# A mixture-of-experts and attention kernel: one copy placed ahead of an exponential, rows added a step sooner, and four transfers moved to another queue

## The chip, the cores and the metric

The kernel runs on one core of a Trainium2 chip. The metric is device time in microseconds (us) from the start to the end of one execution; lower is better. The page and the rows below come from one execution taken by the hardware profiler. PE is TensorE (matrix products), DVE is VectorE, ACT is ScalarE, POOL is GpSimd, and SP is SyncE, which here only issues DMA transfers.

## The reference

The input `x` has 8 sequences of 1024 tokens with 256 numbers each. It is normalised, and two branches work on the result:

```
xn = layernorm(x)
q, k, v = split(xn @ w_qkv)                    # 16 heads of 64
attn = softmax(causal(q @ k.T / sqrt(64))) @ v @ w_out
ffn  = sum over the two best experts of gate * (relu(xn @ w1[e] + b1[e]) @ w2[e] + b2[e])
out  = x + attn + ffn
```

An expert takes at most 2048 of the 8192 tokens. All is float32. Most products are made of three, of a rounded high part and the rest (`h` and `l` at the end of a tile's name).

## The kernel before

The program has stages one after the other: normalising and routing, the experts (up to about 900 us), and then attention, which adds all parts and is where the whole change lies. Attention runs over 64 **units** (`UNITS`): a unit is one pair of heads of one sequence, so 8 units make a sequence. A unit has 20 **steps**, and every engine goes through (unit, step) in the same order, with semaphores between the engines.

- A unit's 8 rows of 128 queries are done in 5 **rounds** of 4 steps (`ROUNDS`): rows (3,2), (4,1), (5,0), (6), (7). For a row, PE makes the scores S (L1231), DVE masks them, writes them to `pr` and finds the extreme `negm` (L1356), ACT takes the exponential in place (L1294), and a round later DVE makes reciprocals (L1362) and POOL scales the rows (L1438).
- The scaled rows have to be turned before they multiply the values. Rows 0 to 3 are turned by PE in 128x128 blocks into a PSUM bank (L1187), and ACT copies them out to `pT` (L1284). These pieces are called **turns**: `t30`, `t31`, `t20`, `t21` (row, head) and `t1`, `t0`. Rows 4 to 7 are turned by DVE in small squares (L1400, tile `squares`), and then DMA transfers, 16 for each group of two rows, place them in `pT`: `place` on SP's queue (L1085), `place_rest` on POOL's (L1467). Group 2 is rows 4 and 5, group 3 rows 6 and 7. In one unit SP issues 16 transfers of group 2 and 12 of group 3, and POOL 4 of group 3.
- PE multiplies by the values in three runs (L1264): groups 0 and 1, group 2, and group 3, at steps 3, 7 and 15 of the next unit.
- Beside this PE makes other **pieces**, each into one of three shared PSUM banks `W0`, `W1`, `W2`: `p0` to `p3` (queries and keys of the next unit, L1142), `v0`, `v1` (values, L1157), `xn` (L1165), and `o0` to `o3` (output products, L1176). The step of each piece on PE, ACT and DVE, and its bank, are written out by hand in the tables `STEP_OF`, `ACT_STEP`, `DVE_STEP`, `BANK_OF`. A piece waits until the piece before it in the same bank has been read. At steps 8 to 10 the order on PE is `t30` (W1), `t31` (W2), `t20` (W0), `t21` (W1), `o1` (W2), `p1` (W0), `o2` (W1).
- POOL's own work has a table too, `POOL_AT`. `split_w` and `split_wv` divide the next weights in high and low parts; `wvl` of `split_wv`, in every second unit, is what `v0` of the next unit needs, and `wl` lets SP load the next weights. `fetch`, `weigh`, `add` and `total` fetch a token's two expert rows, weigh and add them, and add the sum to `res` (L1502). DVE adds the output products to the same `res` (L1382), so the DVE addition for the same query group waits for `total`.

Of the kernel before, what the change touches and what calls it, by code (L numbers as in the profile page):

```python
# [845 lines left out]
def attention_and_sum(nc, k, x, xn_dram, w_qkv, w_out, pick, y_dram, out, start):  # L846
# [3 lines left out]
    UNITS = BATCH * PAIRS  # L850
# [7 lines left out]
    QUARTERS = P // BL  # L858
# [28 lines left out]
               "t30": 8, "t31": 8, "t20": 8, "t21": 8, "o1": 9, "p1": 10, "o2": 11,  # L887
               "p0": 12, "t1": 13,
               "t0": 16, "p2": 16, "p3": 17, "o3": 18}
    ACT_STEP = {"v0": 2, "xn": 2, "v1": 6, "t30": 8, "t31": 8, "t20": 9, "t21": 9, "p1": 12,  # L890
                "p0": 12, "t1": 13, "t0": 16, "p2": 17, "p3": 18}
    DVE_STEP = {"xn": 3, "o0": 6, "o1": 10, "p1": 12, "o2": 12, "p0": 15, "p2": 19, "p3": 19, "o3": STEPS + 2}
    BANK_OF = {"v0": 0, "xn": 1,
# [15 lines left out]
    RUN_OF = {g: j for j, groups in enumerate(RUN_GROUPS) for g in groups}  # L909
# [6 lines left out]
                return n - later, j  # L916
        return None

    POOL_AT = {"split_w": 1, "place3": 4, "total": 5, "choose": 6, "fetch0": 8, "fetch1": 9, "weigh": 13, "add": 14, "split_wv": 17}

    turns_of = lambda i: [t for t in TURNS if i in [at[0] for at in TURNS[t]]]
    turn_unit = lambda n, t: n if t in STEP_OF else END_STEP[TURNS[t][0][0]][0]
# [21 lines left out]
    with ExitStack() as c:  # L944
# [86 lines left out]
        score, negmax, expd, scaled = (Count(sem(f"s_{n}"), len(ORDER)) for n in ("score", "negmax", "expd", "scaled"))  # L1031
        recip = Count(sem("s_recip"), len(ROUNDS))
        squared = Count(sem("s_squared"), 2 * len(SQUARED))
        placed = {2: Count(sem("s_placed2"), 16 * QUARTERS * QUARTERS), 3: Count(sem("s_placed3"), 16 * QUARTERS * (QUARTERS - 1))}
        pool_placed = Count(sem("s_pool_placed"), 16 * QUARTERS)
        pv = Count(sem("s_pv"), RUNS)
        ohi, olo = Count(sem("s_ohi"), RUNS), Count(sem("s_olo"), RUNS)
        filled = Pieces(sem("s_filled"), lambda name: True)
# [30 lines left out]
        @block.sync  # L1069
        def _(e):  # L1070
            def load_w(m):
                for c_ in range(MC):
                    e.dma_start(wr[:, 2 * c_:2 * c_ + 2], wv[m % PAIRS][:, c_, :, 0:2 * HDIM]).then_inc(wload.sem, 16)

            def load_wv(m):
                for c_ in range(MC):
                    e.dma_start(wvr[:, c_], wvv[m % (PAIRS // 2)][:, c_, :, 2 * HDIM:]).then_inc(wvload.sem, 16)

            def place(n, g):
                e.wait_ge(squared.sem, squared.at(n, 4 * g - 4))  # L1080
                if n > 0:
                    e.wait_ge(pv.sem, pv.at(n - 1, RUN_OF[g] + 1))
                for a in range(QUARTERS - (g == 3)):
                    for b in range(QUARTERS):
                        e.dma_start(*strip(g, a, b)).then_inc(placed[g].sem, 16)  # L1085

            def store(b, g):
                e.wait_ge(dve.sem, dve.at((b + 1) * PAIRS, f"o{g}"))
                e.dma_start(outv[:, b, 2 * g:2 * g + 2], res[:, 2 * g:2 * g + 2]).then_inc(stored[g].sem, 16)

            def refill(b, g):
                if b > 0:
                    e.wait_ge(stored[g].sem, stored[g].at(b - 1, 16))
                e.dma_start(res[:, 2 * g:2 * g + 2], xv[:, b, 2 * g:2 * g + 2]).then_inc(rload[g].sem, 16)

            e.dma_start(xnt[:], xnv[AHEAD]).then_inc(xload.sem, 16)
            load_w(1)
            load_wv(1)
            for n in range(UNITS):
                b, u = n // PAIRS, n % PAIRS  # L1100
                if n == 0:
                    e.wait_ge(s_wolo, 1)
                    for g in range(GROUPS):
                        refill(0, g)
                if n + 2 < UNITS:
                    e.wait_ge(wlo.sem, wlo.at(n, MC))
                    load_w(n + 2)
                if n + 1 + AHEAD < TILES:
                    e.wait_ge(filled.sem, filled.at(n, "xn"))
                    e.dma_start(xnt[:], xnv[n + 1 + AHEAD]).then_inc(xload.sem, 16)  # L1110
                if n > 0:
                    place(n - 1, 3)
                if b > 0 and u == 0:
                    for g in range(3):
                        store(b - 1, g)
                    for g in range(3):
                        refill(b, g)
                if n < UNITS - 1:
                    place(n, 2)
                if n % 2 == 0 and n // 2 + 2 < UNITS // 2:  # L1120
                    e.wait_ge(wvlo.sem, wvlo.at(n // 2, MC))
                    load_wv(n // 2 + 2)
                if b > 0 and u == 0:
                    store(b - 1, 3)
                    refill(b, 3)
            for g in range(GROUPS):
                store(BATCH - 1, g)
            for g in range(GROUPS):
                e.wait_ge(stored[g].sem, stored[g].at(BATCH - 1, 16))

        @block.tensor
        def _(e):
# [103 lines left out]
            def values(n, j):  # L1236
                groups = RUN_GROUPS[j]
                if in_squares(n, 2 * groups[0]):
                    g = groups[0]
                    e.wait_ge(placed[g].sem, placed[g].at(n + 1, 0))  # L1240
                    if g == 3:
                        e.wait_ge(pool_placed.sem, pool_placed.at(n + 1, 0))
                else:
                    for m, name in [(turn_unit(n, t), t) for g in groups for i in (2 * g, 2 * g + 1) for t in turns_of(i)]:
                        if by_act(name):
                            e.wait_ge(act.sem, act.at(m, name))
                        else:
                            e.wait_ge(dve.sem, dve.at(m, name))
                if j == 0:
                    e.wait_ge(act.sem, act.at(n // 2 * 2 - 1, "v1"))  # L1250
                    if n > 0:
                        e.wait_ge(olo.sem, olo.at(n - 1, RUNS))
                else:
                    e.wait_ge(act.sem, act.at(n // 2 * 2, "v1"))
                    e.wait_ge(olo.sem, olo.at(n, j))
                for g in groups:
                    KT, o0 = 2 * g + 2, g % 2 * GQ
                    for kt in range(KT):
                        a = P if kt == KT - 1 else 0
                        for h in range(2):  # L1260
                            hs = slice(h * HDIM, (h + 1) * HDIM)
                            vs = slice(n % 2 * P + h * HDIM, n % 2 * P + (h + 1) * HDIM)
                            turned_p = wide_of(g, h, kt, a // P) if in_squares(n, 2 * g) else pT[g][:, h, kt, a:GQ]
                            ins = e.matmul(O[hs, o0 + a:o0 + GQ], vv[n // 2 % 2][:, kt, vs], turned_p,  # L1264
                                           start=(kt == 0), stop=(kt == KT - 1))
                ins.then_inc(pv.sem, 1)
# [73 lines left out]
        def _(e):  # L1340
# [52 lines left out]
            def square(n, i, h):  # L1393
                g, KT = i // 2, i + 1
                if n > 0 and i % 2 == 0 and h == 0:
                    e.wait_ge(placed[g].sem, placed[g].at(n, 0))
                    if g == 3:
                        e.wait_ge(pool_placed.sem, pool_placed.at(n, 0))
                e.wait_ge(scaled.sem, scaled.at(n, SCALE_ORDER.index((i, h)) + 1))
                e.transpose(sq[g][:, :, 2 * h + i % 2, 0:KT, :],  # L1400
                            room_of(n, i, h)[:, OFFSET[i]:OFFSET[i] + KT * P].rearrange("p (k b i) -> p b k i", b=QUARTERS, i=BL)
                            ).then_inc(squared.sem, 1)
# [30 lines left out]
        def _(e):  # L1433
# [25 lines left out]
                for c_ in range(MC):  # L1459
                    e.tensor_tensor(wvl[:, c_], flat(wvr[:, c_]), wvh[:, c_].bitcast(F32), ALU.subtract).then_inc(wvlo.sem, 1)  # L1460

            def place_rest(n):
                e.wait_ge(squared.sem, squared.at(n + 1, 0))
                if n > 0:
                    e.wait_ge(pv.sem, pv.at(n - 1, RUN_OF[3] + 1))
                for b in range(QUARTERS):
                    e.dma_start(*strip(3, QUARTERS - 1, b)).then_inc(pool_placed.sem, 16)  # L1467

            def choose(m):
                if m > 0:  # L1470
# [35 lines left out]
            for n, s in ALL + END:  # L1506
                r, x = s // SUB, s % SUB
                m, q = back(n, s, SUB)[0], (r - 1) % len(ROUNDS)
                if x == 0 and 0 <= m < UNITS:
                    for j in range(FIRST[q], FIRST[q + 1]):  # L1510
                        scale(m, j)
                for name, at in POOL_AT.items():
                    if s != at:
                        continue
                    if name == "total" and n > 0:
                        total(n - 1)
                    if n == UNITS:
                        continue
                    if name == "place3" and n > 0:
                        place_rest(n - 1)  # L1520
                    elif name == "choose":
                        choose(n)
                    elif name == "split_w" and n + 1 < UNITS:
                        split_w(n)
                    elif name == "split_wv" and n % 2 == 0 and n // 2 + 1 < UNITS // 2:
                        split_wv(n // 2)
                    elif name[:5] == "fetch":
                        fetch(n, int(name[5]))
                    elif name == "weigh":
                        weigh(n)  # L1530
                    elif name == "add":
                        add(n)
# [38 lines left out]
```

## Time and profile before

| | |
|---|---|
| median of 3 runs | 2953.59 us (2950.54 to 2953.61) |
| profiled execution | 2948.78 us, its span 2947.0 us |
| mean granted PE clock | 0.989 of full speed |
| busy share PE / DVE / ACT / POOL | 96% / 71% / 58% / 55% |
| DMA | 371.58 MB, mean 126 GB/s |

The span runs from the first to the last instruction; the profiled execution's own time has 1.8 us more around it. A busy share is a mean over all stages. A timeline row gives the start, the length, and in square brackets the idle time of the engine just before it and what ended it. PE's products overlap, so the distance of two starts tells more of them than their length.

### The profile page before, as it was taken

The numbers are of one execution on the slowest core, as the hardware profiler recorded it, in microseconds if no ns is written. First come the engines' busy times: TensorE is split into PE (matmuls) and PEld (weight loads), VectorE is DVE, ScalarE is ACT, GpSimd is POOL, SyncE is SP. The second block draws the span as 40 slices with busy tenths as digits, with TensorE's granted clock in tenths as the row PEclk, the third lists the DMA queues.
The fourth block names the chain that finished last, engine by engine and source line by source line (L and its number), as shares of the span: only waits on it lengthen the run. The fifth ranks groups of instructions, "written<-read, shape, count | busy, mean of one in ns | idle before, by whom it ended". The sixth has DMA issues, their size and how long they took to land.

```text
span 2947.0 us, 61139 instructions
## 1 busy us (share of the span) xinstructions
PE 2825.5 (96%) x21321; PEld 2283.0 (77%) x21321; DVE 2091.7 (71%) x4448; ACT 1699.5 (58%) x3934; POOL 1606.8 (55%) x2379
## 2 busy tenths in 40 slices
PE   4599999999998999999999999999999999999998
PEld 3489999899997777777777777777777777777776
DVE  7843444434435888888888888888888888888886
ACT  3455444444444666666666666666666666666664
POOL 3122122221214767667667767667667767767674
PEclk8799999999999999999999999999999999999999
DMA  7022212222113555655655655565566557556553
GB/s 252 19 78 76 74 49 80 74 76 66 55 53 102 141 144 146 167 145 153 163 140 150 158 150 153 134 167 152 134 167 156 137 139 184 134 139 179 135 133 93
DMA packets 252806, 371.58 MB, mean 126 GB/s; under 512 B 77392, under 2 KB 177744, under 8 KB 252512
## 3 DMA queue, kind: packets, MB, share of 16 engines
q1 hardware_dynamic: 228096, 301.09, 38.5%
q0 software_dynamic: 24416, 66.65, 8.4%
q8 instruction: 174, 2.85, 0.4%
q14 instruction: 120, 0.98, 0.1%
HBM read 102.80 MB, written 33.55 MB: 46 GB/s over the span
## 4 chain that ended last, share of the span: by engine, by line
PE 62%; SPq 2%; DMA 2%; issue 1%; DVE 1%; ACT 1%; DVEq 0%; ACTq 0%
PE O L1264 17%; PE S L1231 15%; PE W L1142 12%; PE W L1157 7%; PE W L1176 6%; PE W L1187 5%; SPq L1085 2%; DMA pT<-squares 1%; DVE pr L1356 1%; DMA out<-res 0%; ACT pr L1294 0%; PE W L1165 0%; DVE squares L1400 0%; ACT pT L1284 0%; DVE res L1382 0%
## 5 line engine op out<-in xcount | busy, mean ns | idle before, releaser
L1438 POOL TENSOR_SCALAR pr<-pr,rinv 128x512 f32<-128x512 f32 (+7 forms) x1024 | 752.0, 750 | 535.1 <-DVE rinv L1362 528.9
L1294 ACT ACTIVATE pr<-pr,negm 128x512 f32<-128x512 f32 (+7 forms) x1024 | 786.7, 773 | 285.2 <-DVE negm L1356 285.2
L1356 DVE CUSTOM_DVE_ANT_0 pr<-S,late 128x512 f32<-128x512 f32 (+7 forms) x1024 | 717.5, 752 | 109.1 <-PE S L1231 107.6
L1264 PE MATMUL O<-pT,vv 128*64 128x256 f32 (+1 forms) x5120 | 540.3, 362 | 4.6 <-DMA pT<-squares 4.6
L1400 DVE STREAM_TRANSPOSE squares<-pr 128x640 f32<-128x640 f32 x504 | 495.0, 1020 | 0.0
L1264 PEld LDWEIGHTS O<-pT,vv 128*64 128x64 f32 x5120 | 345.8, 137 | 183.1 <-issue 18.9
L832 DVE TENSOR_TENSOR hl<-h,hh 128x512 fp32r<-128x512 f32 x256 | 192.7, 753 | 320.3 <-ACT hh L793 308.1
L789 ACT ACTIVATE h<-pH,b1c 128x512 f32<-128x512 f32 x256 | 176.0, 688 | 367.3 <-PE pH L719 336.9
L1284 ACT ACTIVATE pT<-W 128x512 f32<-128x512 f32 (+3 forms) x520 | 199.2, 437 | 214.8 <-PE W L1187 214.8
L731 PE MATMUL pY<-w2h,hh 128*128 128x256 f32 x1024 | 287.7, 281 | 2.5 <-DVE hl L832 2.5
L731 PE MATMUL pY<-w2l,hh 128*128 128x256 f32 x1024 | 288.9, 282 | 0.0
L731 PE MATMUL pY<-w2h,hl 128*128 128x256 f32 x1024 | 287.9, 281 | 0.0
L1142 PE MATMUL W<-xnh,wh 128*128 128x512 f32 x512 | 221.2, 432 | 23.5 <-issue 18.3
L1382 DVE TENSOR_TENSOR res<-W,res 128x512 f32<-128x512 f32 x256 | 175.7, 686 | 69.0 <-POOL res L1502 44.9
L1231 PE MATMUL S<-khf,qh 64*128 64x512 f32 (+2 forms) x1024 | 218.8, 422 | 2.8 <-DVE negm L1356 2.8
L719 PE MATMUL pH<-xh,w1h 128*128 128x512 f32 x512 | 205.5, 401 | 4.8 <-DVE xl L804 2.6
L1142 PE MATMUL W<-xnh,wl 128*128 128x512 f32 x512 | 202.5, 395 | 0.0
L1142 PE MATMUL W<-xnl,wh 128*128 128x512 f32 x512 | 202.3, 395 | 0.0
L719 PE MATMUL pH<-xl,w1h 128*128 128x512 f32 x512 | 201.7, 394 | 0.0
L719 PE MATMUL pH<-xh,w1l 128*128 128x512 f32 x512 | 201.5, 393 | 0.0
L1294 ACT ACTIVATION_READ_ACCUMULATOR pr<-pr,negm 128x1 f32 x1024 | 199.2, 195 | 0.0
L731 PEld LDWEIGHTS pY<-w2h,hh 128*128 128x128 f32 x1024 | 192.9, 188 | 7.9 <-issue 2.9
(176 smaller groups left out, 6221.7 us busy)
## 6 DMA issues: line engine op xcount, KB each, us to landing
pT<-squares SPq DMA_DIRECT2D x1008, 96.0 KB, 2.1
pT<-squares SPq DMA_DIRECT2D x756, 128.0 KB
pT<-squares POOLq DMA_DIRECT2D x252, 128.0 KB
y<-yb SPq DMA_DIRECT2D x128, 128.0 KB, 1.7
wr<-in_L_attn_w_qkv SPq DMA_DIRECT2D x128, 128.0 KB, 2.3
x<-in_L_attn_x SPq DMA_DIRECT2D x16, 512.0 KB, 9.1
xn<-xn SPq DMA_DIRECT2D x16, 512.0 KB, 4.4
w1r<-in_L_ffn_w SPq DMA_DIRECT2D x8, 1024.0 KB
```

Source lines behind the costliest of these rows:

```text
L719: ins = e.matmul(pH[hc % 4][:], w[par][:, m, ws], xx[q][:, m, :], start=(n == 0), stop=(n == 3 * MC - 1))
L731: ins = e.matmul(pY[t % 2][:], hs[q][:, hc, ts_], ws[par][:, hc, :], start=(hc == 0 and n == 0), stop=(hc == HC - 1 and n == 2))
L832: e.tensor_tensor(hl[q][:, hc, :], h32[hc % 2][:], hh[q][:, hc, :].bitcast(F32), ALU.subtract).then_inc(hlo.sem, 1)
L1142: ins = e.matmul(W, ws[:, 2 * m + of_k], xs[:, t0:t0 + HT, m, :], start=(i == 0), stop=(i == 3 * MC - 1))
L1157: ins = e.matmul(W[:, t * VW:(t + 1) * VW], xs[:, t0 + t, m, :], ws[:, m, :], start=(j == 0), stop=(j == len(terms) - 1))
L1231: ins = e.matmul(S[h][:, off + f * HALF:off + f * HALF + cols], t[hs, i * P:(i + 1) * P], u[f][n % 2][hs, 0:cols], start=(j == 0), stop=(j ...
L1264: ins = e.matmul(O[hs, o0 + a:o0 + GQ], vv[n // 2 % 2][:, kt, vs], turned_p, start=(kt == 0), stop=(kt == KT - 1))
L1284: ins = e.activation(dst, src, ACT.Copy) if by_act(name) else e.tensor_copy(dst, src)
L1294: e.activation(p, p, ACT.Exp, bias=negm[:, c0:c0 + 1], scale=-1.0, accum_out=rsum[:, c0:c0 + 1]).then_inc(expd.sem, 1)
L1356: e.tensor_tensor_reduce(room_of(n, i, h)[:, off:off + w], S[h][:, off:off + w], late[:, SEQ - w:], 1.0, -MASKED, ALU.add, ALU.min, negm[: ...
L1400: e.transpose(sq[g][:, :, 2 * h + i % 2, 0:KT, :], room_of(n, i, h)[:, OFFSET[i]:OFFSET[i] + KT * P].rearrange("p (k b i) -> p b k i", b=Q ...
L1438: e.tensor_scalar(p, p, rinv[:, c0:c0 + 1], 1.0, ALU.mult, ALU.mult).then_inc(scaled.sem, 1)
```

## The change

Three numbers of hand-written tables change, and one function takes over four transfers.

- ACT's step for `t20` goes from 9 to 8, which puts that copy ahead of the first exponential of round (5,0).
- POOL does `total` at step 4 and `place3` at step 5 (before, the other way round).
- A new entry `place2` at step 16 lets POOL issue the last four of group 2's transfers; SP's `place` then issues 12 of both groups. The two places that waited for POOL's transfers of group 3 wait for those of group 2 likewise.

```diff
-    ACT_STEP = {"v0": 2, "xn": 2, "v1": 6, "t30": 8, "t31": 8, "t20": 9, "t21": 9, "p1": 12,
+    ACT_STEP = {"v0": 2, "xn": 2, "v1": 6, "t30": 8, "t31": 8, "t20": 8, "t21": 9, "p1": 12,
...
-    POOL_AT = {"split_w": 1, "place3": 4, "total": 5, "choose": 6, "fetch0": 8, "fetch1": 9, "weigh": 13, "add": 14, "split_wv": 17}
+    POOL_AT = {"split_w": 1, "total": 4, "place3": 5, "choose": 6, "fetch0": 8, "fetch1": 9, "weigh": 13, "add": 14, "place2": 16, "split_wv": 17}
...
-                for a in range(QUARTERS - (g == 3)):
+                for a in range(QUARTERS - 1):
                     for b in range(QUARTERS):
                         e.dma_start(*strip(g, a, b)).then_inc(placed[g].sem, 16)
...
                     e.wait_ge(placed[g].sem, placed[g].at(n + 1, 0))
-                    if g == 3:
-                        e.wait_ge(pool_placed.sem, pool_placed.at(n + 1, 0))
+                    e.wait_ge(pool_placed[g].sem, pool_placed[g].at(n + 1, 0))
...
-            def place_rest(n):
-                e.wait_ge(squared.sem, squared.at(n + 1, 0))
+            def place_rest(n, g):
+                e.wait_ge(squared.sem, squared.at(n, 4 * g - 4))
                 if n > 0:
-                    e.wait_ge(pv.sem, pv.at(n - 1, RUN_OF[3] + 1))
+                    e.wait_ge(pv.sem, pv.at(n - 1, RUN_OF[g] + 1))
                 for b in range(QUARTERS):
-                    e.dma_start(*strip(3, QUARTERS - 1, b)).then_inc(pool_placed.sem, 16)
+                    e.dma_start(*strip(g, QUARTERS - 1, b)).then_inc(pool_placed[g].sem, 16)
```

On ACT, at steps 7 to 9 of the third unit, a row reads: line, operation, what it writes and reads (W0 to W2 are the shared banks, `pr` the rows), and the size. Before:

```order
L1325 ACTIVATE oh<-O 128x256
L1284 ACTIVATE pT1<-W1 128x4x128
L1284 ACTIVATE pT1<-W2 128x4x128
L1294 ACTIVATE pr0,rsum<-pr0,negm 128x768
L1284 ACTIVATE pT1<-W0 128x3x128
L1284 ACTIVATE pT1<-W1 128x3x128
L1294 ACTIVATE pr1,rsum<-pr1,negm 128x768
```

And after the change:

```order
L1324 ACTIVATE oh<-O 128x256
L1283 ACTIVATE pT1<-W1 128x4x128
L1283 ACTIVATE pT1<-W2 128x4x128
L1283 ACTIVATE pT1<-W0 128x3x128
L1293 ACTIVATE pr0,rsum<-pr0,negm 128x768
L1283 ACTIVATE pT1<-W1 128x3x128
L1293 ACTIVATE pr1,rsum<-pr1,negm 128x768
```

The copy out of W0 (`t20`) has passed one exponential of 768 columns; the copy out of W1 (`t21`) has stayed behind it.

On POOL, from the scaling of row 6 (896 columns) in a unit with `split_wv` to the next unit's step 6, before:

```order
L1438 TENSOR_SCALAR pr3<-pr3,rinv 128x896
L1457 TENSOR_SCALAR wvh<-wvr 128x256 x2
L1460 TENSOR_TENSOR wvl<-wvr,wvh 128x256 x2
L1438 TENSOR_SCALAR pr4<-pr4,rinv 128x1024
...
L1438 TENSOR_SCALAR pr1<-pr1,rinv 128x384
L1467 DMA pT3<-squares3 32x1024 x4
L1502 TENSOR_TENSOR res<-res,yg0 128x256
L1472 COPY sel<-pick 128x4
```

After the change, the same places in the program (the second part one unit earlier, where it reads the same):

```order
L1436 TENSOR_SCALAR pr3<-pr3,rinv 128x384
L1500 TENSOR_TENSOR res<-res,yg0 128x256
L1465 DMA pT3<-squares3 32x1024 x4
L1470 COPY sel<-pick 128x4
...
L1436 TENSOR_SCALAR pr3<-pr3,rinv 128x896
L1465 DMA pT2<-squares2 32x768 x4
L1455 TENSOR_SCALAR wvh<-wvr 128x256 x2
L1458 TENSOR_TENSOR wvl<-wvr,wvh 128x256 x2
L1436 TENSOR_SCALAR pr4<-pr4,rinv 128x1024
```

Four transfers of group 2 now stand between the scaling of row 6 and `split_wv`, and the addition to `res` has passed the four transfers of group 3.

## Rows read from the trace of the kernel before

**Rows 1.** The page, part 1: busy us (share of the span) and instructions
```profile
PE 2825.5 (96%) x21321; PEld 2283.0 (77%) x21321; DVE 2091.7 (71%) x4448; ACT 1699.5 (58%) x3934; POOL 1606.8 (55%) x2379
```

**Rows 2.** Waits from 928 to 2885 us: us in total, times, longest
```profile
DVE res L1382 <- POOL res L1502: 44.9, 16, 3.1
...
PE W L1142 <- issue: 18.3, 58, 0.3
...
PEld W L1176 <- ACT pT L1284: 11.1, 62, 0.2
...
PE O L1264 <- DMA pT<-squares: 4.6, 6, 1.8
```

**Rows 3.** Timeline of PE, the end of o1 and the start of p1
```profile
2031.16 0.28 PE L1176 MATMUL W<-woh,ol 128*128 128x256 f32 x1
2031.76 0.51 PE L1142 MATMUL W<-xnh,wh 128*128 128x512 f32 x1 [0.32 <-issue]
2032.11 0.39 PE L1142 MATMUL W<-xnl,wh 128*128 128x512 f32 x1
2032.34 0.40 PE L1142 MATMUL W<-xnh,wl 128*128 128x512 f32 x1
```

**Rows 4.** Timeline of ACT at the same steps
```profile
2029.33 1.09 ACT L1284 ACTIVATE pT<-W 128x512 f32<-128x512 f32 x2 [1.80 <-PE W L1187]
2030.30 0.94 ACT L1294 ACTIVATE pr<-pr,negm 128x768 f32<-128x768 f32 x1
...
2031.22 0.87 ACT L1284 ACTIVATE pT<-W 128x384 f32<-128x384 f32 x2
```

**Rows 5.** Timeline of PE, where v1 ends and o0 begins
```profile
2023.59 0.28 PE L1157 MATMUL W<-wvh,xnl 128*128 128x256 f32 x1
2023.70 0.28 PE L1176 MATMUL W<-woh,oh 128*128 128x256 f32 x1
```

**Rows 6.** Timeline of PE, first product of p1 in three units
```profile
2000.38 0.50 PE L1142 MATMUL W<-xnh,wh 128*128 128x512 f32 x1 [0.32 <-issue]
...
2660.52 0.50 PE L1142 MATMUL W<-xnh,wh 128*128 128x512 f32 x1 [0.32 <-issue]
...
2691.68 0.50 PE L1142 MATMUL W<-xnh,wh 128*128 128x512 f32 x1 [0.32 <-issue]
```

**Rows 7.** Line L1165 (xn): durations ns, first and last start
```profile
L1165 PE MATMUL W<-ident,xnt x110: 270/271/273, 921.2 to 2615.6; 128*128 128x128 f32 x110
```

**Rows 8.** Timeline of POOL around the places of the change
```profile
2011.28 0.78 POOL L1457 TENSOR_SCALAR wvh<-wvr 128x256 fp32r<-128x256 f32 x2
2012.14 1.45 POOL L1460 TENSOR_TENSOR wvl<-wvr,wvh 128x256 fp32r<-128x256 f32 x2
2017.10 2.23 POOL L1438 TENSOR_SCALAR pr<-pr,rinv 128x1024 f32<-128x1024 f32 x2 [3.51 <-DVE rinv L1362]
...
2019.79 0.78 POOL L1447 TENSOR_SCALAR wh<-wr 128x256 fp32r<-128x256 f32 x2
...
2024.98 2.09 POOL L1467 DMA_DIRECT2D pT<-squares  x4
2027.09 0.75 POOL L1502 TENSOR_TENSOR res<-res,yg 128x256 f32<-128x256 f32 x1
```

**Rows 9.** Timeline of DVE beside them
```profile
2011.36 1.23 DVE L1356 CUSTOM_DVE_ANT_0 pr<-S,late 128x1024 f32<-128x1024 f32 x1 [0.86 <-PE S L1231]
...
2013.65 2.10 DVE L1400 STREAM_TRANSPOSE squares<-pr 128x896 f32<-128x896 f32 x2
2015.68 0.65 DVE L1390 TENSOR_TENSOR ql<-W,qh 128x512 fp32r<-128x512 f32 x1
```

**Rows 10.** Timeline of PE, first product of v0
```profile
2016.43 0.39 PE L1157 MATMUL W<-wvh,xnh 128*128 128x256 f32 x1
```

**Rows 11.** Timeline of SP's queue: issues of groups 2 and 3
```profile
2008.25 10.23 SPq L1085 DMA_DIRECT2D pT<-squares  x16
...
2023.61 8.33 SPq L1085 DMA_DIRECT2D pT<-squares  x12
```

**Rows 12.** Issues from 928 us on, line L1085: us from issue to landing
```profile
DMA to landing us min/median/max: 2.0/2.1/3.9
```

**Rows 13.** Timeline of PE, first products with group 3's rows
```profile
2037.55 0.65 PE L1264 MATMUL O<-pT,vv 128*64 128x256 f32 x4
```

More of the change, by code:

```diff
@@ L1033, in attention_and_sum @@
         squared = Count(sem("s_squared"), 2 * len(SQUARED))
-        placed = {2: Count(sem("s_placed2"), 16 * QUARTERS * QUARTERS), 3: Count(sem("s_placed3"), 16 * QUARTERS * (QUARTERS - 1))}
-        pool_placed = Count(sem("s_pool_placed"), 16 * QUARTERS)
+        placed = {2: Count(sem("s_placed2"), 16 * QUARTERS * (QUARTERS - 1)), 3: Count(sem("s_placed3"), 16 * QUARTERS * (QUARTERS - 1))}
+        pool_placed = {g: Count(sem(f"s_pool_placed{g}"), 16 * QUARTERS) for g in (2, 3)}
         pv = Count(sem("s_pv"), RUNS)
@@ L1396, in square @@
                     e.wait_ge(placed[g].sem, placed[g].at(n, 0))
-                    if g == 3:
-                        e.wait_ge(pool_placed.sem, pool_placed.at(n, 0))
+                    e.wait_ge(pool_placed[g].sem, pool_placed[g].at(n, 0))
                 e.wait_ge(scaled.sem, scaled.at(n, SCALE_ORDER.index((i, h)) + 1))
@@ L1519, in _ @@
                     if name == "place3" and n > 0:
-                        place_rest(n - 1)
+                        place_rest(n - 1, 3)
+                    elif name == "place2" and n < UNITS - 1:
+                        place_rest(n, 2)
                     elif name == "choose":
```

## The prediction

> **What bounds the kernel now.** I read the page's busy shares first. PE is busy 96% of the span, the next engine, DVE, 71% [rows 1]. So time can only come from what PE still waits for, or from PE having less to do. The list of waits over the units of attention (928 to 2885 us) says how little that is [rows 2]: 18.3 us before L1142 in 58 places, put down to "issue"; 11.1 us of PE's weight loads before L1176, ended by a copy of ACT; 4.6 us before L1264 for the placing transfers. The longest wait of the four is DVE's: 44.9 us in 16 places for POOL's addition to `res`.
>
> Is PE the chain from unit to unit, so that a wait removed there shortens every unit? The trace has an experiment of its own. The piece `xn`, two small PE products, is there in 55 units and then no more: its last start is 2615.6 [rows 7]. The first product of `p1` stands 31.38 us apart in two units with it (2000.38 and 2031.76) and 31.16 apart in two without it (2660.52 and 2691.68) [rows 3, 6]. Two products less shorten the unit by 0.22 us, about two distances of 0.11 between such starts. PE's own time passes into the period one to one; nothing else holds a unit at 31.4.
>
> Then I looked at the 18.3 us in the timeline. The last product of `o1` starts at 2031.16, the first of `p1` at 2031.76 [rows 3]. `p1` writes bank W0, and the last user of W0 was `t20`, which ACT has to copy out. ACT copies `t30` and `t31` from 2029.33 on, does an exponential of 768 columns at 2030.30, and only at 2031.22 begins on `t20` and `t21`, two copies in 0.87 us [rows 4]. Half of that puts the end of `t20`'s copy near 2031.66, and PE starts 0.10 us later. The "issue" is this wait: each of the gaps of 0.32 stands at this place.
>
> **ScalarE's copy.** Moved ahead of the exponential, `t20`'s copy starts where the exponential did, at 2030.30, and ends near 2030.8. PE needs it at about 2031.3, so the wait is gone with 0.5 us to spare. What comes back: where a piece follows another with its waits fulfilled, the starts are 0.11 apart (2023.59 to 2023.70, the last of `v1` to the first of `o0`) [rows 5]. Here they are 0.60 apart, so 0.48 to 0.49 comes back. The first product after the gap costs more as well: 0.35 to the second, 0.23 from there to the third [rows 3], so another 0.11 to 0.12 if the stream isn't broken. Together 0.59 us in each unit with a `p1`, 63 units. The lower bound for this term is what the list counts as idle, 18.3 us in all [rows 2]; I take the distances of starts, since PE's ends are modelled and its starts are not.
>
> What is late instead? The first exponential ends some 0.45 us later. Behind it stands `t21`'s copy, which now alone follows it and so ends where it did, near 2032.1; the second exponential starts as before. `o2`, which needs W1 from `t21`, comes six products of 0.23 after `p1`, so from about 2032.7 on: 0.6 us of cover. The round's reciprocals wait for all its exponentials, and the last has not moved.
>
> **Does the gain stay?** PE comes 0.59 us earlier to everything behind `p1`. The next wait that could catch it is group 3's run at 2037.55 [rows 13]. SP issues these transfers until 2031.94 (2023.61 + 8.33) [rows 11], and they land 2.1 us later [rows 12], at about 2034.0. That leaves 3.5 us, of which the change takes 0.59. At the borders between sequences, where SP stores and reloads `res` too, there is no room: the 4.6 us in 6 places are just these [rows 2]. There are 7 borders. At each the 0.59 us is given back as a longer wait for group 3, whose issues begin with the squares of row 7, which nothing moves. So 63 - 7 = 56 units count: 56 x 0.59 = 33.0 us. DVE's part of the loop, from the scores of row 7 to `v0`, is tight (`ql` runs until 2016.33, `v0` starts at 2016.43 [rows 9, 10]), but it begins after an idle 0.86 us that PE's scores end, so it moves with PE.
>
> **The sum of expert rows.** `total` now runs 2.09 us sooner, the length of the four issues that it passes [rows 8]. DVE's 44.9 us in 16 places, 2.8 each, shrink to about 0.7 each, 34 us of DVE's time in all. PE gets nothing of it: the list shows no wait of PE for these additions, and the gap before `p1` is there all the same. Value 0, hidden under PE's products. Group 3's four transfers of POOL start 0.75 us later [rows 8], at 2025.7, and are issued by 2027.9, still 4 us ahead of SP's last. Cost 0.
>
> **Four transfers of group 2 to POOL.** SP's 16 issues of 10.23 us become 12, so it is done 2.5 us sooner; group 2's run had been waiting for nothing. Value 0 in most units. POOL pays four issues: beside other DVE work they took 2.09 us [rows 8]. They fall behind the scaling of row 6, from 2011.3 to 2013.4, and group 2's squares have long been there (SP began on them at 2008.25 [rows 11]). Behind them stand `split_wv` in 31 units and the scaling of row 7. `split_wv` takes 2.31 us and ended at 2013.59; now 2015.7, while `v0` needs it at 2016.43: 0.7 us of cover is left. Row 7's scaling waits for DVE until 2017.10 anyway, with 3.51 us idle before it. Cost 0, but the cover is thin.
>
> The profile has no plain issue of POOL beside DVE's squares of row 6. From below, 0 us on the path at 2.09 us for the four. From above, POOL may be held until DVE's unbroken run ends, 2013.65 + 2.10 = 2015.75 [rows 9]. What speaks against the upper end: two small POOL operations at 2011.28 beside DVE's minimum took 0.78 us, the same as two of their size at 2019.79 beside other DVE work [rows 8, 9]. I take 2.09. The Trainium skill has a rule that speaks against this edit: "SBUF — State Buffer", section "SBUF: two separate sides", says that a DMA issued from GpSimd has its descriptors written by that engine, which is locked out of the shared port while VectorE runs an operation in a two-port mode, so that the transfer seems blocked by it. By that rule the sum would be that of the last rival below, if DVE's operations here are of that kind; by the rows it is 33.0 us gained.
>
> **The sum.** 33.0 + 0 + 0. The profiled execution took 2948.8 us, so its like would be 2915.8. The median of the runs shown is 4.8 above it, so against that 2953.6 - 33.0 = 2920.6; I say 2920.
>
> **The rivals.**
> - Only the counted idle comes back, because `p1`'s first product stays slow: 18 us, 2935. For it: the first product of `p1` may need its pause for another reason. Against it: [rows 5]. Chance 0.13.
> - More comes back. SP's four issues fewer and the DMA queue emptied sooner also take away the waits at the borders: 63 x 0.59 + 4.6 = 42 us, 2912. Against it: at a border SP waits for stores of `res` in between, so it reaches group 3 no sooner. Chance 0.13.
> - The gap moves. PE comes sooner and stands before group 3's run in all units, or another chain holds the period. That needs transfers landing 3 us later than now, or a chain that the step of 0.22 with `xn` would have shown. Time within 3 us of 2952. Chance 0.08.
> - Slower: POOL's four issues are held by DVE. They end at 2015.75, `split_wv` at 2018.06, `v0` is 1.7 us late in 31 units: 53 us lost against 33 gained, 2974. It decides from a price of 3.9 us for the four issues on (2.84 us from the end of `wvl` to `v0`, and 33 / 31 = 1.06 more). Chance 0.07.
>
> My forecast has 0.55, between 2915 and 2926; 0.04 is left to mixtures, mostly on the fast side.
>
> **How the numbers follow.** A measurement of this kernel tells about 0.2%, 6 us, from no change. Faster: 0.55 + 0.13 + 0.13 and 0.03 of the mixtures, 0.84. Same 0.09, slower 0.07. The range takes in the first three cases, from 2910 to 2937, and leaves out some 0.2.
>
> **What would show it.** Right: in the profile after, `p1` starts 0.11 to 0.12 after the last product of `o1`, its second product 0.23 later, the "issue" row before L1142 has shrunk from 18.3 us to nearly nothing, and units are 30.8 us apart. PE's wait for group 3 at the borders is longer, 4.6 + 7 x 0.59, about 9 us. DVE's wait for `total` is near 11 us. POOL's eight plain issues in a unit take about 0.52 us each, and SP issues 12 and 12. Wrong: a wait before L1157 ended by POOL's `wvl` (issues dear), a wait before L1264 in most units (gap moved), or `p1` still 0.2 us or more behind `o1` (the first rival).

## The result and the profile after

| | before | after |
|---|---|---|
| median | 2953.6 us (4 runs, 2950.5 to 2957.3) | 2912.0 us (4 runs, 2911.6 to 2915.7) |
| profiled execution, its span | 2948.8, 2947.0 us | 2915.7, 2913.9 us |

The ratio is 0.9864, with a 95% interval of 0.9849 to 0.9878: 1.4% faster, 41.6 us by the medians. The profiled execution of after is the slowest of its four, so between the two profiled ones the gain is 33.1 us by their spans.

The kernel's lines from L1264 on stand one or two lines higher after the change (values are L1263, ACT's copies L1283, POOL's issues L1465). First the page's part 1, which answers to [rows 1]:

```profile
PE 2814.5 (97%) x21321; PEld 2284.1 (78%) x21321; DVE 2084.7 (72%) x4448; ACT 1699.7 (58%) x3934; POOL 1723.0 (59%) x2631
```

PE has the same 21321 instructions. POOL is busier by 116 us; its issues alone by 127 us (258.8 us for 504 against 131.8 us for 252).

The timeline of PE at the end of `o1` and the start of `p1`, and `p1`'s first product one unit later:

```profile
2015.51 0.28 PE L1176 MATMUL W<-woh,ol 128*128 128x256 f32 x1
2015.63 0.39 PE L1142 MATMUL W<-xnh,wh 128*128 128x512 f32 x1
2015.86 0.40 PE L1142 MATMUL W<-xnl,wh 128*128 128x512 f32 x1
...
2046.46 0.39 PE L1142 MATMUL W<-xnh,wh 128*128 128x512 f32 x1
```

The first product of `p1` is 0.12 us behind `o1`, where it was 0.60 [rows 3], and the second 0.23 behind the first, where it was 0.35. The unit is 30.83 us long instead of 31.38.

ACT at the same steps (answers to [rows 4]):

```profile
2013.67 1.47 ACT L1283 ACTIVATE pT<-W 128x512 f32<-128x512 f32 x3 [1.80 <-PE W L1187]
2015.01 0.95 ACT L1293 ACTIVATE pr<-pr,negm 128x768 f32<-128x768 f32 x1
2015.84 0.21 ACT L1293 ACTIVATION_READ_ACCUMULATOR pr<-pr,negm 128x1 f32 x1
2015.93 0.50 ACT L1283 ACTIVATE pT<-W 128x384 f32<-128x384 f32 x1
2016.30 0.95 ACT L1293 ACTIVATE pr<-pr,negm 128x768 f32<-128x768 f32 x1
```

Three copies in a row, done at 2015.14, 0.5 us before PE needs the third. `t21`'s copy and the second exponential follow without a hole.

The waits of the units of attention (928 to 2855 us; us in total, times, longest), answering to [rows 2]:

```profile
DVE res L1381 <- POOL res L1500: 10.1, 15, 1.0
...
PE O L1263 <- DMA pT<-squares: 3.1, 2, 1.8
...
PE S L1231 <- DVE negm L1355: 2.5, 2, 1.4
PE W L1157 <- POOL wvl L1458: 2.0, 1, 2.0
...
PE W L1187 <- issue: 0.7, 1, 0.7
PE W L1142 <- ACT pT L1283: 0.3, 1, 0.3
```

The 18.3 us of "issue" before L1142 are gone. DVE's wait for `total` fell from 44.9 to 10.1 us. The wait for group 3 stands at 2 borders with 3.1 us, not at more of them with 9. One wait is new: 2.0 us for POOL's `wvl`, in the first unit.

Where the 33.1 us of the two profiled spans are: from the first `p1` that both traces record behind `o1` to the last, 61 units, 1918.6 us before and 1880.9 after, 37.7 less. Of these 36.0 are 61 times 0.59, and 1.7 are waits at the borders between sequences. Behind it nothing changed (68.3 and 68.1 us). Ahead of it 4.7 us were lost: that `p1` starts at 964.83, before at 960.08. The busy times by stage show why (busy us of each engine with its count, granted PE clock, DMA share, GB/s), the first row of before and the second of after:

```profile
900.00:960.00 60.00, 50.29 (x373) 39.24 (x371) 39.58 (x96) 35.03 (x89) 33.92 (x54) 1.00 0.48 124
```
```profile
900.00:960.00 60.00, 49.43 (x337) 38.54 (x337) 37.10 (x86) 32.50 (x82) 32.68 (x53) 0.94 0.41 116
```

PE's granted clock was 1.00 there before and 0.94 after: part of the stretch ran at the lower level of 1.2 GHz, in a stage where PE waits for the first pieces. The 4.7 us have three parts. PE's first product of attention starts at 904.15 instead of 903.22, so 0.9 us were late before the changed code. 1.2 us are `v0` of the first unit (below). The other 2.6 us are two places where the clock was down, by the timelines of PE: from 908.63 to 914.66 the same work took 6.03 us at a granted clock of 0.73, where before it took 4.54 us at 1.00 (907.69 to 912.23); from 948.40 to 964.83 it took 16.43 us at 0.90, where before it took 15.28 at 1.00 (944.80 to 960.08).

### The profile page after: what moved, and what is told of

It is laid out like the page before. It is cut to its first block, busy times and chain, and to the rows that moved or that the text cites. A ratio compares the mean times of both kernels' runs of the same rounds, so it can differ in the third digit from the quotient of the medians.

```text
span 2913.9 us, 61264 instructions
## 1 busy us (share of the span) xinstructions
PE 2814.5 (97%) x21321; PEld 2284.1 (78%) x21321; DVE 2084.7 (72%) x4448; ACT 1699.7 (58%) x3934; POOL 1723.0 (59%) x2631
## 4 chain that ended last, share of the span: by engine, by line
PE 66%; DVE 1%; SPq 1%; DMA 0%; issue 0%; ACT 0%; POOL 0%; DVEq 0%; ACTq 0%
PE O L1263 18%; PE S L1231 16%; PE W L1142 12%; PE W L1157 7%; PE W L1176 7%; PE W L1187 6%; SPq L1085 1%; DVE pr L1355 0%; PE W L1165 0%; DMA pT<-squares 0%; DVE squares L1398 0%; ACT pr L1293 0%; DMA out<-res 0%; ACT pT L1283 0%; DVE res L1381 0%
## 5 line engine op out<-in xcount | busy, mean ns | idle before, releaser
L1263 PE MATMUL O<-pT,vv 128*64 128x256 f32 (+1 forms) x5120 | 541.3, 362 | 3.1 <-DMA pT<-squares 3.1
L1398 DVE STREAM_TRANSPOSE squares<-pr 128x640 f32<-128x640 f32 x504 | 494.8, 1020 | 0.0
L1263 PEld LDWEIGHTS O<-pT,vv 128*64 128x64 f32 x5120 | 346.4, 137 | 181.8 <-issue 20.4
L1283 ACT ACTIVATE pT<-W 128x512 f32<-128x512 f32 (+3 forms) x520 | 199.6, 437 | 215.8 <-PE W L1187 215.8
L1465 POOL DMA_DIRECT2D pT<-squares x504 | 258.8, 521 | 0.3 <-issue 0.2
L1142 PE MATMUL W<-xnh,wh 128*128 128x512 f32 x512 | 215.1, 420 | 3.0 <-DVE klf L1389 1.5
L664 POOL COPY idx<-slot_token 128x4 uint32 (+1 forms) x30 | 8.8, 293 | 335.3 <-PE pX L705 335.3
L1142 PE MATMUL W<-xnl,wh 128*128 128x512 f32 x512 | 203.2, 397 | 0.0
L1142 PE MATMUL W<-xnh,wl 128*128 128x512 f32 x512 | 203.1, 397 | 0.0
```

Source lines behind the costliest of these rows:

```text
L1142: ins = e.matmul(W, ws[:, 2 * m + of_k], xs[:, t0:t0 + HT, m, :], start=(i == 0), stop=(i == 3 * MC - 1))
L1398: e.transpose(sq[g][:, :, 2 * h + i % 2, 0:KT, :], room_of(n, i, h)[:, OFFSET[i]:OFFSET[i] + KT * P].rearrange("p (k b i) -> p b k i", b=Q ...
L1465: e.dma_start(*strip(g, QUARTERS - 1, b)).then_inc(pool_placed[g].sem, 16)
```

## The experiments

Twelve kernels ran in three groups of four; each group shares the runs of the kernel before on its chip, with medians of 2952.2, 2952.6 and 2954.5 us. "Period" is the distance from one unit's `p1` to the next; the border waits are the sum of what periods exceed their median by, over the 7 borders. "By the list" is the total of the rows `PE O <- DMA pT<-squares` in the view of waits. The first measure also takes in whatever else makes a border's unit longer, a lower clock for one.

### The parts alone

`copy_only` takes only the number for ScalarE; `total_only` only the swap on POOL; `copy_total` both; `place2_only` only the four transfers:

```diff
-    ACT_STEP = {... "t20": 9, ...}             # copy_only, copy_total
+    ACT_STEP = {... "t20": 8, ...}
-    POOL_AT = {... "place3": 4, "total": 5, ...}   # total_only, copy_total
+    POOL_AT = {... "total": 4, "place3": 5, ...}
+    POOL_AT = {... "place2": 16, ...}          # place2_only, with its waits
```

**copy_only.** 

> Only ScalarE's step for t20 goes from 9 to 8; POOL's table and the issues are as before. Theory A (the copy is the whole gain in every unit, and the four issues on POOL are what kept the border waits small): p1 stands 0.12 us behind o1, units are 30.8 us apart, PE's waits for group 3 at the borders grow from 4.6 to about 9 us; 33 us faster than before, 2920 us. Rival B (the border waits have nothing to do with the four issues): they stay near 3 to 5 us as in the changed kernel, and this is 38 to 41 us faster, 2912 to 2915 us.

Measured: 2920.2 us, ratio 0.9896 (0.9879 to 0.9913). Period 30.81, `p1` 0.12 behind `o1`, border waits 10.0 us at all 7 borders.

```profile
PE O L1264 <- DMA pT<-squares: 9.6, 7, 2.2
```

As theory A had it: 32 us by the medians (31 by the ratio) where 33 were forecast, and the border waits doubled, from 4.9 us.

**place2_only.** 

> Only the four transfers of group 2 go to POOL; the copy and the addition stay where they were. Theory A: units stay 31.4 us apart with p1 0.60 us behind o1; the border waits shrink from 4.6 us to near 0, and the first unit loses about 2 us because v0 waits for wvl there; together 1 to 4 us faster, 2950 to 2953 us. Rival B: the border waits stay near 4.6 us and the time is 2953 to 2956 us. If POOL's issues were dear, v0 would wait in 31 units and the time would be over 2970 us.

Measured: 2951.0 us, ratio 0.9997 (0.9988 to 1.0005), no difference. Period 31.39. Border waits 0.75 us, at one border, where the kernel before has 4.9; `v0` of the first unit starts 2.6 us after the scores ahead of it, before 1.1. The two small effects of theory A are both there: 4.1 us gained, 1.5 lost. What is left of them, 2.6 us, is too little for this measurement to tell from nothing.

**total_only.** 

> Only total and place3 change places in POOL's table. Both theories: DVE's wait for POOL's addition falls from 44.9 us to about 10 us and PE shows nothing of it: 2953.6 us within 3 us, ratio 1.000 within 0.001. A third view, that DVE's waits reach PE after all, would give 10 us or more.

Measured: 2952.9 us, ratio 1.0003 (0.9994 to 1.0012). DVE's wait fell as expected and gave nothing:

```profile
DVE res L1382 <- POOL res L1502: 10.8, 16, 1.0
```

**copy_total.** 

> The changed kernel without its four issues of group 2: the copy and the addition moved. Theory A: as with the copy alone, 2920 us, border waits about 9 us, and the first unit free of the wait for wvl. Rival B: 2912 us or less.

Measured: 2923.7 us, ratio 0.9904 (0.9889 to 0.9919), border waits about 9 us with a period of 30.81. As with the copy alone. By the medians the parts don't add up: the copy gives 32 us, the four transfers alone 1, the addition less than nothing (0.7 us slower), and all of it 41.6, some 9 more than the sum. The traces show a small part of the 9: the four transfers take 4.1 us of border waits off the kernel before, and 5.5 to 6.8 beside the copy (10.0 to 4.5 or 3.2). What makes the rest is not shown.

### One suspected cost doubled

**copy_later.** The copies of `t20` and `t21` behind both exponentials:

```diff
-    ACT_STEP = {... "t20": 8, "t21": 9, ...}
+    ACT_STEP = {... "t20": 10, "t21": 10, ...}
```

> The changed kernel with the copies of t20 and t21 behind both exponentials of row 5 (step 10). Theory (p1 waits for t20's copy, and PE's waits pass into the period one to one): the copy ends about 1.2 us later than in the kernel before, p1 stands 1.8 us behind o1 and units are about 32.6 us apart; 63 x 1.75 = 110 us slower than the changed kernel, some 3020 us. Rival (part of it is taken up because other chains have slack): less than half of that, under 2970 us.

Measured: 3011.4 us, ratio 1.0195 (1.0181 to 1.0209). `p1` is 1.51 us behind `o1` and the period 32.33, so 1.52 us more than after the change. The timeline of PE names the releaser:

```profile
2032.49 0.28 PE L1176 MATMUL W<-woh,ol 128*128 128x256 f32 x1
2033.99 0.50 PE L1142 MATMUL W<-xnh,wh 128*128 128x512 f32 x1 [1.23 <-ACT pT L1283]
```

63 x 1.52 = 96 us, measured 99 against 2912. I had put the copy 0.3 us too late, hence 3020. What PE waits at this place passes into the time whole; the rival (less than half) fell.

**eight_issues.** POOL issues eight of group 2's transfers, SP eight:

```diff
-                for a in range(QUARTERS - 1):
+                for a in range(QUARTERS - (4 - g)):
...
-                for b in range(QUARTERS):
-                    e.dma_start(*strip(g, QUARTERS - 1, b)).then_inc(pool_placed[g].sem, 16)
+                for a in range(QUARTERS - (4 - g), QUARTERS):
+                    for b in range(QUARTERS):
+                        e.dma_start(*strip(g, a, b)).then_inc(pool_placed[g].sem, 16)
```

> The changed kernel with eight instead of four transfers of group 2 issued by POOL, and eight by SP. Theory (0.52 us for each issue, 0.74 us of cover to v0): wvl ends 2.1 us later, v0 waits 1.4 us in 31 units, 43 us lost: about 2955 us, and the list names PE W L1157 <- POOL wvl. Rival (PE finds time elsewhere, so v0's wait is taken back within the unit): 2912 to 2925 us. A third view, that fewer issues on SP matter more than anything: faster than 2912 us.

Measured: 2958.4 us, ratio 1.0015 (1.0006 to 1.0024): with four issues more the whole gain is gone. The list of waits, and the timelines of POOL and PE at one `v0`:

```profile
PE W L1157 <- POOL wvl L1458: 43.9, 31, 3.9
```
```profile
2147.56 4.05 POOL L1466 DMA_DIRECT2D pT<-squares  x8
2151.62 0.80 POOL L1455 TENSOR_SCALAR wvh<-wvr 128x256 fp32r<-128x256 f32 x2
2152.51 1.41 POOL L1458 TENSOR_TENSOR wvl<-wvr,wvh 128x256 fp32r<-128x256 f32 x2
```
```profile
2154.07 0.36 PE L1157 MATMUL W<-wvh,xnh 128*128 128x256 f32 x1 [1.25 <-POOL wvl L1458]
```

Eight issues last 4.05 us and PE waits in 31 units, 43.9 us by the list where 43 were expected. This is the prediction's slow rival, reached by the number of issues instead of their price.

### Why the four transfers help at the borders

SP's issues at one border (start, length, what, count), first with the copy alone, then in the changed kernel:

```profile
1930.47 10.03 SPq L1085 DMA_DIRECT2D pT<-squares  x16
1940.55 1.20 SPq L1077 DMA_DIRECT2D wvr<-in_L_attn_w_qkv  x2
1941.79 1.47 SPq L1089 DMA_DIRECT2D out<-res  x1
1945.24 0.37 SPq L1094 DMA_DIRECT2D res<-in_L_attn_x  x1
1945.65 0.98 SPq L1073 DMA_DIRECT2D wr<-in_L_attn_w_qkv  x2
1946.68 0.47 SPq L1110 DMA_DIRECT2D xnt<-xn  x1
1947.24 8.38 SPq L1085 DMA_DIRECT2D pT<-squares  x12
```
```profile
1931.28 7.54 SPq L1085 DMA_DIRECT2D pT<-squares  x12
1938.87 1.19 SPq L1077 DMA_DIRECT2D wvr<-in_L_attn_w_qkv  x2
1942.50 0.38 SPq L1089 DMA_DIRECT2D out<-res  x1
1944.65 0.37 SPq L1094 DMA_DIRECT2D res<-in_L_attn_x  x1
1945.07 0.98 SPq L1073 DMA_DIRECT2D wr<-in_L_attn_w_qkv  x2
1946.09 0.47 SPq L1110 DMA_DIRECT2D xnt<-xn  x1
1946.65 8.54 SPq L1085 DMA_DIRECT2D pT<-squares  x12
```

With 16 issues SP is still busy when DVE has finished `o3`, and the store of `res` stands at once behind the loads. The reload waits until the store has landed, 3.45 us after the store's issue began, and group 3's issues follow 2.00 us behind the reload. With 12 issues SP stands ready for 2.4 us, issues the store as DVE ends, and the store lands in 2.15 us. Two things could be at work: SP's time, or the bytes in the queue ahead of the store. One experiment is for each part of the chain.

**wv_behind.** The copy alone, and on SP the load of `wvr` behind the store and the reload:

```diff
+                if b > 0 and u == 0:
+                    store(b - 1, 3)
+                    refill(b, 3)
                 if n % 2 == 0 and n // 2 + 2 < UNITS // 2:
                     e.wait_ge(wvlo.sem, wvlo.at(n // 2, MC))
                     load_wv(n // 2 + 2)
-                if b > 0 and u == 0:
-                    store(b - 1, 3)
-                    refill(b, 3)
```

> Only the copy is moved, and on SP the load of the next wvr is issued behind the store and reload of res's last quarter, not ahead of them. Theory (at a border the store comes too late because of what SP issues ahead of it, and the reload and group 3 follow it): the store is issued up to 1.2 us sooner, the border waits of 10.0 us with the copy alone shrink to 3 to 6 us, 2914 to 2917 us. Rival (only the transfers of group 2 in SP's queue hold the store's bytes up, not the issues): waits stay near 10 us, 2920 us.

Measured: 2925.7 us, ratio 0.9910 (0.9894 to 0.9925); border waits 9 us, 9.5 us by the list in 8 places. My theory fell as I had put it. The store was now issued as soon as DVE was done, at all seven borders, and the reload 0.6 to 1.9 us sooner, but the two issues of `wvr` then stood ahead of group 3, which followed 3.1 us behind the reload instead of 2.0. They had only changed places in the chain. The store also landed sooner at each of the seven borders, 2.1 to 3.6 us after its issue against 2.7 to 3.8 with the copy alone (one profile each), so the loads ahead of it in the queue seem to count as well. The rival, which put that down to group 2's transfers alone, named the right waits; this run doesn't decide on it.

**place2_behind.** The changed kernel, the four issues after `split_wv`:

```diff
-    POOL_AT = {... "place2": 16, "split_wv": 17}
+    POOL_AT = {... "split_wv": 17, "place2": 17}
```

> The changed kernel with POOL's four issues of group 2 placed behind split_wv instead of ahead of it. Theory (the four issues cost the path only where v0 stands right behind wvl, which is in the first unit): the cover between wvl and v0 goes back from 0.74 to 2.8 us, the first unit gets back 1.3 us or so, the border waits stay small: 2910 to 2912 us, 1 to 2 us faster than the changed kernel. Rival (the place among POOL's work sets what the borders gain): the border waits return and it is 2915 us or more.

Measured: 2915.1 us (2911.1 to 2922.0), ratio 0.9866 (0.9851 to 0.9881), the same as the changed kernel within the interval. In its profile `v0` of the first unit is back at 0.6 us, as with the copy alone, but the border waits are 9 us again, 7.9 by the list in 6 places. SP's issues were as few, and yet the stores took 2.5 to 4 us to land: in the changed kernel it was 2.1 to 2.2 at five borders. So the expectation of small border waits was wrong, and the rival, that the place among POOL's work sets them, had both the waits and 2915 us. It is not shown by that: the profiled execution is the slowest of the four, at 2922.0 us. And 1.7 of the 9 us are the clock's: at the first border the run of products behind the wait took 5.15 us where it takes 3.46, at a granted clock of 0.93 from 1200 to 1225 us.

**copy_refill, after_refill, behind_refill.** The reload of `res`'s last quarter goes behind group 3's transfers of the next unit, so that these wait for no store; once on the copy alone, once on the changed kernel, once on place2_behind. **after_again** is the changed kernel beside them.

```diff
                 if n > 0:
                     place(n - 1, 3)
+                if b > 0 and u == 1:
+                    refill(b, 3)
...
                 if b > 0 and u == 0:
                     store(b - 1, 3)
-                    refill(b, 3)
```

> The changed kernel once more, beside the other three of this group: 2912 us, border waits of 0 to 3 us, and v0 of the first unit late.

> Only the copy is moved, and SP reloads the last quarter of res at a border behind group 3's transfers instead of ahead of them, so that these no longer wait for the store to land. Theory (chain at a border: SP's issues, store, its landing, reload, group 3): group 3's first issue comes 2 us sooner than with the copy alone, the 10.0 us of border waits are gone, 2910 us. Rival (the DMA engines are simply full at a border, whatever the order): waits of 5 us or more stay, 2915 to 2920 us.

> The changed kernel with the same reload behind group 3. Theory: its border waits (3.2 us in the profile shown) go to 0 and the rest is as it was: 2909 to 2911 us. Rival (the reload now delays something else): 2912 us or more.

> As the one before, and POOL's four issues of group 2 behind split_wv. Theory: no border waits whichever place the four issues have, and v0 of the first unit 1.3 us earlier: 2908 to 2910 us, the fastest of all. Rival (the place of the four issues sets the border waits by itself): 2915 us as before.

| kernel | median us | ratio (95%) | border waits us | first v0 behind the scores |
|---|---|---|---|---|
| after_again | 2913.5 | 0.9863 (0.9848 to 0.9878) | 4.5 | 2.3 |
| copy_refill | 2910.6 | 0.9854 (0.9839 to 0.9869) | 0 | 0.6 |
| after_refill | 2912.3 | 0.9860 (0.9845 to 0.9875) | 0 | 2.3 |
| behind_refill | 2910.3 | 0.9849 (0.9836 to 0.9863) | 0 | 0.6 |

SP in copy_refill, at the same border as above:

```profile
1936.17 0.51 SPq L1089 DMA_DIRECT2D out<-res  x1
1938.38 0.88 SPq L1073 DMA_DIRECT2D wr<-in_L_attn_w_qkv  x2
1939.30 0.47 SPq L1110 DMA_DIRECT2D xnt<-xn  x1
1939.87 8.12 SPq L1085 DMA_DIRECT2D pT<-squares  x12
1948.04 0.59 SPq L1094 DMA_DIRECT2D res<-in_L_attn_x  x1
```

Group 3 follows 3.7 us behind the store, before it was 5.5, and the border waits are 0 with the old 16 issues on SP as well. So it was the wait for the store in SP's queue, and neither full DMA engines nor the place of the four issues by itself. The edit does a second thing, though: it takes the reload's 256 KB out of the time in which group 3 is on its way. Counted from the `p1` ahead of it, SP reaches group 3 1.9 to 2.7 us sooner at six borders than with the copy alone, more than the wait at each of them (at most 2.3). At the first it is only 0.1 us sooner, and 0.7 us of wait is gone as well; there the bytes may be what counts. No run parts the two.

With this one edit the copy alone does as well as all three edits of the change: 2910.6 against 2913.5 beside it. behind_refill has the lowest median of all kernels here, but the intervals of these four overlap, so only "no slower than the changed kernel" is shown. Two expectations were missed. after_again's border waits were to be 0 to 3 us and are 4.5; the waits themselves are 2.8 by the list, and 1.7 are again the clock's at the first border (5.11 us for the run of products, 0.93). after_refill was to be 2909 to 2911 us and is 2912.3, where the rival began: its border waits are gone as expected, but the time differs from after_again by 1.2 us only, which is inside the noise.

## Why the prediction was right, step by step

- **PE's waits pass into the period one to one, and the gap before `p1` is ACT's copy.** Right. 0.60 became 0.12, the second product came at 0.23 instead of 0.35, the period went from 31.4 to 30.8. The term of 0.59 a unit is 0.58 to 0.59 in the trace; copy_later shows the same slope the other way: against after, the gap is 1.39 us longer, the product behind it 0.11, and the period 1.52. The first rival, of 18 us, is out. Its size, and the lower bound of the term, left out a second row of the same list for the same place, so the idle time counted before `p1` was 20.8 us and not 18.3:

```profile
PE W L1142 <- ACT pT L1284: 2.5, 5, 1.2
```

   One of these five is the first unit's, and there the gain did not stay: the gap before its `p1` fell from 1.24 to 0.32 us, and PE's next wait for DVE grew from 0.31 to 1.08.
- **`t21`'s copy and the second exponential stay where they were.** Right, by the rows of ACT.
- **The sum of expert rows is worth nothing.** Right: total_only 1.0003, with 34 us of DVE's waiting gone.
- **Four issues cost 2.09 us and are covered.** Right in 30 of 31 units: 2.11 us in the trace, and 0.74 us left between `wvl` and `v0` (0.7 forecast). Wrong in the first, where the units aren't in step yet and there is no such cover. The timeline of POOL there, and of PE:

```profile
943.84 2.12 POOL L1465 DMA_DIRECT2D pT<-squares  x4
945.98 0.79 POOL L1455 TENSOR_SCALAR wvh<-wvr 128x256 fp32r<-128x256 f32 x2
946.85 1.41 POOL L1458 TENSOR_TENSOR wvl<-wvr,wvh 128x256 fp32r<-128x256 f32 x2
```
```profile
948.40 0.36 PE L1157 MATMUL W<-wvh,xnh 128*128 128x256 f32 x1 [1.96 <-POOL wvl L1458]
```

   The distance from the scores to this `v0` was 1.07 us before and 2.30 after, 1.2 us lost.
- **POOL isn't held by DVE.** The issues take 521 ns in the mean over 504, before 528 over 252, now also beside DVE's minimum of row 7. The case for which the prediction had no row, issues beside the squares of row 6, is in eight_issues: there eight issues run from 2147.56 to 2151.61, DVE's squares (L1398) from 2149.96 on, and an issue takes 0.51 us all the same. The rule of the Trainium skill ("SBUF — State Buffer", "SBUF: two separate sides") is not contradicted, since no run here shows that DVE's operations at this place use a two-port mode; its effect doesn't occur here.
- **At the seven borders the gain is given back, since nothing moves group 3's issues.** This is the term that was mis-sized: "SP waits for stores of `res` in between, so it reaches group 3 no sooner". Measured from the last `p1` ahead of it, SP reaches it 1.3 to 1.9 us sooner than with the copy alone at six of seven borders (1.5 us later at the first), because the store is issued and lands earlier. For the copy alone the term was exact: 33.0 us forecast, 32.0 measured, border waits 10.0 where 9 were forecast. With the four transfers the border waits are 3.2 and 4.5 us in the two profiles of the changed kernel. The profiled executions of copy_only and of the changed kernel are 4.5 us apart, and this accounts for it: 6.8 us less at the borders, and 2.7 lost ahead of the first `p1` behind `o1`, of which 1.7 are `v0` of the first unit (2.30 us behind the scores against 0.64). The medians are 8.2 apart. The other 3.7 us lie between the profiled execution of the changed kernel, its slowest, and the rest, of which there is no trace; the 2.6 us that the lower clock took in that profile may be part of it, which is not shown. So the case that came is the second rival, "more comes back", with its mechanism and 2912 us, at which I had put 0.13; 2912.0 lies just outside the 2915 to 2926 of my own forecast.
- **The 33.1 us between the two profiled spans are the forecast's 33.0 by luck.** At the borders 5.8 us more came back than I had put (3.2 where 9 were forecast), and 4.7 us were lost at the start of attention, which the forecast didn't have.
- **How long group 3's transfers take to land was misread.** The 2.1 us of [rows 12] is group 2's alone. The page's list of issues has this landing for the transfers of 96 KB, and none for group 3's of 128 KB:

```profile
pT<-squares SPq DMA_DIRECT2D x1008, 96.0 KB, 2.1
pT<-squares SPq DMA_DIRECT2D x756, 128.0 KB
```

   In the kernel before, at the six borders where PE waits for group 3, its run starts 4.5 to 6.2 us behind the start of SP's last issue. So the 3.5 us of room in a plain unit were too many. The sum doesn't change, since after the change no plain unit waits there.

Open: at the first two borders the store still takes 3.2 to 4.3 us to land in the changed kernel, and the waits stay. What the DMA engines do there that they don't at the other five, no run tells. That POOL's place for the four transfers changes the landing of the stores (place2_behind) is seen in one profile only. Why all three edits together give some 9 us more than the sum of their medians is open too, but for the part above.

## What to carry to other kernels

Where one engine is busy 96% and everything else follows it, look for the distances of its starts, not only its idle rows: a gap listed as 0.32 us of "issue" was worth 0.59. An edit that measures as nothing alone may be worth more beside another: the four transfers gave 1 us by themselves and 8 beside the copy, by the medians. Part of it is that the copy had taken up slack and made the waits at the borders twice as long; here the traces show only 1 to 3 us of that, so such a difference has to be looked up in the rows before it is believed. And in a queue that issues in order, look at what waits for a landing: moving one issue behind the transfers that the bottleneck needs did as much as taking a quarter of a group's issues off that queue.

## What I had not expected of the hardware

- The landing of one 256 KB store took from 2.1 to 4.3 us at the same place in the program, in one execution of the changed kernel: 4.3 and 3.2 us at the first two borders and 2.1 to 2.2 at the other five. With the copy alone, where SP's issues stand close ahead of it, it took 2.7 to 3.8.
- At the start of attention the granted PE clock differs between executions: 1.00 from 900 to 960 us in the profile of before, 0.94 and 0.97 in two profiles of the changed kernel. PE was busy 50.3, 49.4 and 49.4 of these 60 us. It costs up to about 3 us, and since two profiles of one kernel differ in it, it says nothing about the change. The same happened later in two profiles (after_again, place2_behind): PE had waited 2.1 and 2.3 us for group 3 at the first border, and the run of products behind it took 5.1 us instead of 3.46.
